# 16-head attention: TensorE's step for the next sequence's operands stands behind the diagonal scores, ahead of the values

## The chip, the cores and the metric

The kernel runs on one core of a Trainium2 chip. Its engines are TensorE (PE, with its weight loads shown apart as PEld), VectorE (DVE), ScalarE (ACT), GpSimd (POOL) and SyncE (SP), each with a program of its own; they meet at semaphores. The metric is the device time of one execution in microseconds (us). Of the kernel before, three runs gave 1028.70, 1028.92 and 1029.70 us, median 1028.92.

## The reference

Two transformer layers work on x of shape (8, 512, 128), each an attention and a feed-forward part with a normalisation in front and a gate behind. The change lies in the attention of the second layer, which has 16 heads of 8 channels:

```python
qkv = (x @ w_qkv.T + b_qkv).reshape(B, T, 3, H, dh)          # q, k, v per head
std_logits = einsum('bhqd,bhkd->bhqk', q, k) * scale
write_lines, read_lines = exterior(w1, w2), exterior(r1, r2)  # 6 numbers per head, divided by their norm
incidence = einsum('bqhp,bkhp->bhqk', read_lines, write_lines @ J6)
bias = incidence * decays ** (q - k) * (q > k) * bias_scale
attn = softmax(std_logits + bias, causal)
out  = einsum('bhqk,bhkd->bqhd', attn, v) @ w_out.T + b_out
```

## The kernel before, in words

The attention runs over 128 heads in a row (8 sequences of 16 heads). One pass of the loop over n is called slot n here; there are 152 slots (`LAST`), and a slot's place in its sequence is n mod 16. In slot n each engine works on head n for the maxima and on head j = n - 8 for the exponentials. TensorE's slot, in program order (lines 1728 to 1771):

1. `on_diagonal(n)` (L1630, L1631, L1633): scores on the diagonal. It waits until VectorE has weighted the incidences of head n (`weigh`, L1777).
2. `values` (L1693, waits for the exponentials), `turn_out` (L1701), and once per sequence `turn_rows` (L1716) and `project` (L1722). `values` comes in slots 1, 2 and 3 of every four, `turn_out` in slot 0 of every four, for groups of four heads.
3. `incidences_by_key(j)` (L1649). It waits for the exponentials of head j - 1 (L1858); VectorE's `weigh_by_key(j)` (L1782) waits for it.
4. `side(n)`: TensorE's step for the operands of the next sequence, one step of the generator `operands_pe`.
5. `below(n)` (L1641), `incidences(n + 1)` (L1623; VectorE's `weigh(n + 1)` waits for it), `on_diagonal_by_key(j)` (L1656 to L1659; it waits for `weigh_by_key(j)`, and ScalarE's exponentials L1857 and L1858 wait for it), `below_by_key(j + 1)` (L1668), `turn_maxima` (L1675).

VectorE's slot is `weigh(n)` L1777, maxima L1795, L1796, L1787, `weigh_by_key(j)` L1782, `normalise` L1808 and L1812, `residual` L1819, and its own side step last. ScalarE's side step stands first in its slot, GpSimd's near the front.

The operands of sequence b are made from slot 16b - 27 on. TensorE's steps with work in them, by n mod 16:

| n mod 16 | TensorE's step | who takes it |
|---|---|---|
| 9 | transposes of the normalised x (L1250) | ACT L1350 |
| 10, 11 | q, k (L1254, L1257) | ACT L1356, then POOL L1417, L1419 |
| 12 | v (L1261) | ACT L1361 |
| 13, 14 | line coordinates (L1271, L1272) | ACT L1369 (cp), then POOL L1434 on |
| 5 | transposes of half the lines (L1286), waits for GpSimd's L1402 | ACT L1375, then DVE L1326, in the same slot |
| 7 | transposes of the other half (L1286) | ACT L1378, then DVE L1330, L1331, in the same slot |

Between slot 14 and slot 5 GpSimd makes the lines from cp and divides them by their norms: products L1434 and L1435, differences L1442 to L1447, squares and sums L1451 to L1461, one VectorE hop (L1309, L1311, in VectorE's side step of slot 2 mod 16), Newton steps L1393 to L1397, product L1402. In the same program order it also does L1922, L1930 and L1907 to L1915. Sequences 0 and 1 are prepared in the first layer, except for the two L1286 steps of sequence 1 (slots 5 and 7). In the loop TensorE's side step therefore has work in 50 slots; 48 of them lie behind slot 8, that is behind the first `incidences_by_key`.

Of the kernel before, what the change touches and what calls it, by code (L numbers as in the profile page):

```python
# [36 lines left out]
def over(ap, n):  # L37
    return ap.rearrange("p (o c) -> p o c", o=1).to_broadcast([ap.shape[0], n, ap.shape[1]])
# [984 lines left out]
def attention1(c, t, sh, held):  # L1023
# [111 lines left out]
    def group_at(n, after):  # L1135

        q, r = divmod(n - after - G - LAG, G)
        return q if r == 0 and 0 <= q < GROUPS_ else None
# [8 lines left out]
    def rows_at(n, after):  # L1147
        return next((b for b in range(B) if rows_slot(b) + after == n), None)
# [426 lines left out]
    def main(late, behind):  # L1575
# [27 lines left out]
        def on_pe():  # L1603
            def block(x, n, a):

                i, h = place(n)
                return x[i][:, h * T + a * P:h * T + (a + 1) * P]
# [6 lines left out]
            def incidences(n):  # L1614


                if n % G == 0:
                    pe.wait_ge(s_fetch[n // G % RING], 64 * (n // H + 1))
                if n:
                    pe.wait_ge(s_ra, n)  # L1620
                for a in range(NT):
                    for z in HALVES:
                        m = pe.matmul(psD[z, a * P + HB:(a + 1) * P], block(QO, n, a)[:, z], block(KC, n, a)[:, z], start=a == 0, stop=False, skip_group_check=True)  # L1623
                m.then_inc(s_inc, 1)

            def on_diagonal(n):
                pe.wait_ge(s_wq, n + 1)
                for a in range(NT):
                    q, k = block(QO, n, a), block(KB, n, a)
                    pe.matmul(psD[HB:P, a * P:(a + 1) * P], q[:, HB:P], k, start=False, stop=False, skip_group_check=True)  # L1630
                    pe.matmul(psD[0:HB, a * P + HB:(a + 1) * P], q[:, 0:HB], k[:, 0:HB], start=False, stop=False, skip_group_check=True)  # L1631
                for z in HALVES:
                    m = pe.matmul(half(psD[z, :], 1), sh.identh[:, z], over(maskq, NT), start=False, stop=True, skip_group_check=True)  # L1633
                m.then_inc(s_own, 1)

            def below(n):
                if n:
                    pe.wait_ge(s_rc, n)
                i, h = place(n)
                for a, at in ROW_AT.items():  # L1640
                    m = pe.matmul(psX[:, at:at + a * P], block(QO, n, a), KA[i][:, h * KX + off[a]:h * KX + off[a + 1]], start=True, stop=True, skip_group_check=True)  # L1641
                m.then_inc(s_off, 1)

            def incidences_by_key(n):
                if n:
                    pe.wait_ge(s_expd, n)
                for a in range(NT):
                    for z in HALVES:
                        m = pe.matmul(psDT[z, a * P:a * P + HB], block(KC, n, a)[:, z], block(QO, n, a)[:, z], start=a == 0, stop=False, skip_group_check=True)  # L1649
                m.then_inc(s_incT, 1)  # L1650

            def on_diagonal_by_key(n):
                pe.wait_ge(s_wk, n + 1)
                for a in range(NT):
                    q, k = block(QO, n, a), block(KB, n, a)
                    pe.matmul(psDT[0:HB, a * P:(a + 1) * P], k[:, 0:HB], q, start=False, stop=False, skip_group_check=True)  # L1656
                    pe.matmul(psDT[HB:P, a * P:a * P + HB], k[:, HB:P], q[:, HB:P], start=False, stop=False, skip_group_check=True)
                for z in HALVES:
                    m = pe.matmul(half(psDT[z, :], 0), sh.identh[:, z], over(maskk, NT), start=False, stop=True, skip_group_check=True)  # L1659
                m.then_inc(s_ownT, 1)  # L1660

            def below_by_key(n):
                if n % G == 0:
                    pe.wait_ge(s_mset[n // G % 2], 16 * (n // G // 2 + 1))
                if n:
                    pe.wait_ge(s_expo, n)
                for x, (k, a) in enumerate(PAIRS):
                    m = pe.matmul(psXT[:, x * P:(x + 1) * P], decayed(n, k, a), block(QO, n, a), start=True, stop=True, skip_group_check=True)  # L1668
                m.then_inc(s_offT, 1)
# [7 lines left out]
            def values(q, k):  # L1677

                b = q // 4
                if q == 0:  # L1680
                    pe.wait_ge(s_edge, 1)
                if k == 0:
                    pe.wait_ge(s_expd, G * (q + 1))
                    pe.wait_ge(s_expo, G * (q + 1))
                    if q:
                        pe.wait_ge(s_O, q)
                at, first = k * P, NT + sum(NT - 1 - x for x in range(k))
                for c0, c1, e0 in ((at, at + P, at), (at + P, T, first * P)):
                    if c0 < c1:
                        for n in range(G * q, G * q + G):  # L1690
                            h = n % H
                            r, v0 = 32 * (h % 4), (k * H + h) * VH
                            m = pe.matmul(psO[r:r + 32, c0:c1], vv[b % NV][:, v0:v0 + 32], ET[n % NE][:, e0:e0 + c1 - c0],  # L1693
                                          start=c0 == 0, stop=k == NT - 1, skip_group_check=True)
                if k == NT - 1:
                    m.then_inc(s_pv, 1)

            def turn_out(q):
                pe.wait_ge(s_oS, q + 1)
                for i in range(NT):  # L1700
                    m = pe.transpose(psO[:, i * P:(i + 1) * P], oS[:, i * P:(i + 1) * P], sh.ident)  # L1701
                m.then_inc(s_oT, 1)

            def turn_rows(b):
                pe.wait_ge(s_O, 4 * b + 4)

                if b + 3 < B:
                    pe.wait_ge(s_cp, 2 * (b + 3) + 2)
                else:
                    pe.wait_ge(s_rawlo, 2 * B)  # L1710
                if b:
                    pe.wait_ge(s_Y, b)
                if b == B - 1:
                    pe.wait_ge(behind.s_seen, 1)
                for i in range(NT):
                    m = pe.transpose(psA[:, i * P:(i + 1) * P], O[:, i * P:(i + 1) * P], sh.ident)  # L1716
                m.then_inc(s_OT, 1)

            def project(b):
                pe.wait_ge(s_rows, b + 1)  # L1720
                for i in range(NT):
                    m = pe.matmul(psA[:, i * D:(i + 1) * D], oT[:, i * P:(i + 1) * P], wo, start=True, stop=True)  # L1722
                m.then_inc(s_proj, 1)

            side = ahead.pe
            pe.wait_ge(s_place, 1)
            incidences(0)
            for n in range(LAST):
                j = n - LAG
                if n < HEADS:  # L1730
                    on_diagonal(n)
                q = group_at(n, 1)
                if q is not None:
                    values(q, 0)
                q = group_at(n, 2)
                if q is not None:
                    values(q, 1)
                q = group_at(n, 3)
                if q is not None:
                    values(q, 2)  # L1740
                    values(q, 3)
                q = group_at(n, 4)
                if q is not None:
                    turn_out(q)
                b = rows_at(n, 0)
                if b is not None:
                    turn_rows(b)
                b = rows_at(n, 1)
                if b is not None:
                    project(b)  # L1750
                if 0 <= j < HEADS:
                    incidences_by_key(j)
                side(n)
                if n < HEADS:
                    below(n)
                if n + 1 < HEADS:
                    incidences(n + 1)
                if 0 <= j < HEADS:
                    on_diagonal_by_key(j)
                if 0 <= j + 1 < HEADS:  # L1760
                    below_by_key(j + 1)
                g, x = divmod(n - 5, G)
                if x == 0 and 0 <= g < GROUPS_:
                    turn_maxima(g)
                if n == behind.FLAG:

                    pe.wait_ge(s_Y, B - 1)
                if n == behind.ROWS:

                    pe.wait_ge(s_ra, HEADS)  # L1770
                behind.pe(n)
# [160 lines left out]

        on_sp()
        on_pe()
        on_dve()
        on_act()
# [377 lines left out]
```

## Time and profile before

| | |
|---|---|
| median of 3 runs | 1028.92 us (1028.70 to 1029.70) |
| profiled execution, its own time | 1027.37 us |
| its span, first to last instruction | 1026.1 us |
| PE busy | 857.4 us, 84% |
| DVE busy | 741.1 us, 72% |
| ACT busy | 656.5 us, 64% |
| POOL busy | 407.4 us, 40% |
| mean granted TensorE clock | 0.939 of full |

Busy shares are means over stages with different limits. The 16-head attention takes the stretch from about 320 to 830 us. Times in the rows below are counted from the first instruction. A timeline row has the start, the duration, the engine and line, the tiles, and in brackets the idle time of the engine before it and what ended it. Starts of matmul groups are firmer than their ends, so pieces are measured here from start to start. One sequence, slots 62 to 72, is followed throughout.

### The profile page before, as it was taken

How to read it: one execution, taken by the hardware profiler on the slowest of the kernel's cores; microseconds unless marked ns; L12 is line 12 of the kernel's file. 1: busy time of each engine (PE TensorE's matmuls, PEld its weight loads, DVE VectorE, ACT ScalarE, POOL GpSimd, SP SyncE). 2: the span in 40 equal slices, each digit the busy share in tenths (PEclk: the TensorE clock that was granted, in tenths of full speed). 3: DMA queues.
4: the chain of work that ended last, by engine and by line, in shares of the span. 5: the costliest groups of instructions: out<-in, count | busy, mean ns of one | idle time of the engine just before them, and what ended most of it. 6: DMA issues, size and time to landing. Idle time of an engine off the chain costs nothing.

```text
span 1026.1 us, 25492 instructions
## 1 busy us (share of the span) xinstructions
PE 857.4 (84%) x9999; PEld 532.0 (52%) x9999; DVE 741.1 (72%) x1794; ACT 656.5 (64%) x1154; POOL 407.4 (40%) x667
## 2 busy tenths in 40 slices
PE   4688888877376798989989899898898869898987
PEld 2344455545254465666656566565565534444434
DVE  4776888898886777677686867768688456656653
ACT  4668888747144465766666576766566738585865
POOL 3043555456557455384654637355032210101000
PEclk9899999989686699999999999999999989899999
DMA  5000000000333362533425244352532000000000
GB/s 150 22 0 1 1 1 1 1 1 2 106 88 98 78 171 58 133 103 95 127 68 160 62 116 127 76 155 63 150 107 66 2 1 1 21 2 21 1 22 21
DMA packets 70698, 63.60 MB, mean 62 GB/s; under 512 B 30600, under 2 KB 62824, under 8 KB 70576
## 3 DMA queue, kind: packets, MB, share of 16 engines
q1 hardware_dynamic: 70064, 61.90, 23.0%
q8 instruction: 83, 1.36, 0.6%
q14 instruction: 39, 0.32, 0.1%
q10 hardware_dynamic: 512, 0.02, 0.0%
HBM read 34.02 MB, written 27.36 MB: 60 GB/s over the span
## 4 chain that ended last, share of the span: by engine, by line
PE 37%; POOL 10%; DVE 9%; issue 6%; ACT 5%; SPq 1%; DMA 1%; POOLq 0%; DVEq 0%; ACTq 0%
PE bank L2115 12%; PE bank L1693 6%; PE bank L1668 2%; PE bank L1649 2%; PE bank L1641 2%; PE bank L1630 2%; POOL M L1434 2%; ACT 4g L2173 1%; POOL M L1435 1%; DVE bank L1777 1%; DVE 4f L2209 1%; PE bank L1623 1%; PE bank L1633 1%; POOL sq L1451 1%; PE bank L1659 1%
## 5 line engine op out<-in xcount | busy, mean ns | idle before, releaser
L1857 ACT ACTIVATE ET<-bank 64x512 f32<-64x512 f32 x128 | 75.5, 590 | 100.0 <-PE bank L1659 99.2
L2196 DVE TENSOR_TENSOR act<-4f,act 128x512 f16<-128x512 f32 x96 | 66.4, 691 | 57.7 <-ACT act L2163 57.5
L1852 ACT ACTIVATE ET<-bank 128x768 f32<-128x768 f32 x128 | 103.2, 806 | 2.4
L1777 DVE TENSOR_TENSOR bank<-bank,W 128x256 f32<-128x256 f32 x128 | 54.7, 427 | 52.7 <-PE bank L1623 52.7
L1693 PE MATMUL bank<-ET,vv 128*32 128x128 f32 (+2 forms) x1792 | 89.1, 323 | 0.8 <-DVE O L1812 0.8
L1787 DVE TENSOR_REDUCE mo<-bank 128x4 f32<-128x512 f32 x128 | 87.4, 683 | 2.4 <-PE bank L1633 2.3
L1782 DVE TENSOR_TENSOR bank<-bank,WT 128x256 f32<-128x256 f32 x128 | 55.1, 431 | 44.2 <-PE bank L1649 41.1
L2163 ACT ACTIVATE act<-4f 128x512 f16<-128x512 f32 x96 | 60.4, 630 | 28.3 <-DVE 4f L2209 26.2
L1795 DVE TENSOR_REDUCE mo<-bank 128x3 f32<-128x384 f32 x128 | 70.0, 547 | 0.0
L1796 DVE TENSOR_REDUCE mo<-bank 128x3 f32<-128x384 f32 x128 | 70.0, 547 | 0.0
L2115 PE MATMUL bank<-act,std 128*128 128x512 f16 x256 | 58.3, 390 | 0.0
L2115 PE MATMUL bank<-act,cp 128*128 128x512 f16 x256 | 56.5, 379 | 0.0
L1630 PE MATMUL bank<-ring 128*64 128x128 f16 x256 | 28.5, 239 | 32.1 <-DVE bank L1777 32.1
L1693 PEld LDWEIGHTS bank<-ET,vv 128*32 128x32 f32 x1792 | 43.6, 109 | 14.5 <-ACT ET L1858 1.0
L1858 ACT ACTIVATE ET<-bank 64x256 f32<-64x256 f32 x128 | 48.6, 380 | 1.5
L1633 PE MATMUL bank<-maskq,identh 128*64 128x256 bf16 x256 | 49.0, 286 | 0.0
L1434 POOL TENSOR_TENSOR M<-cp 128x192 f32<-128x192 f32 (+2 forms) x48 | 24.2, 505 | 61.6 <-ACT cp L1369 61.6
L1659 PE MATMUL bank<-maskk,identh 128*64 128x256 bf16 x256 | 48.0, 277 | 0.0
L2184 ACT ACTIVATE 4f<-bank,roots 128x512 f32<-128x512 f32 x64 | 43.3, 676 | 7.3 <-PE bank L2115 7.3
L2233 POOL TENSOR_TENSOR X<-X,4Y 128x512 f32<-128x512 f32 x8 | 10.1, 1265 | 91.6 <-DVE 4Y L2222 91.6
L139 POOL TENSOR_TENSOR rstd<-ve,neghalf 128x4 f32<-128x4 f32 x8 | 9.3, 1161 | 92.3 <-DVE ve L121 92.3
L2115 PEld LDWEIGHTS bank<-act,std 128*128 128x128 f16 x256 | 25.7, 101 | 31.4 <-issue 3.3
(384 smaller groups left out, 2544.8 us busy)
## 6 DMA issues: line engine op xcount, KB each, us to landing
ring<-scr_q SPq DMA_DIRECT2D x16, 324.0 KB
QO<-scr_q SPq DMA_DIRECT2D x16, 324.0 KB
ring<-scr_a SPq DMA_DIRECT2D x16, 252.0 KB
KA<-scr_a SPq DMA_DIRECT2D x16, 252.0 KB
ring<-scr_k SPq DMA_DIRECT2D x16, 168.0 KB
KB<-scr_k SPq DMA_DIRECT2D x16, 168.0 KB
scr_a<-dk SPq DMA_DIRECT2D x8, 288.0 KB, 2.6
X<-in_x SPq DMA_DIRECT2D x8, 256.0 KB, 5.1
```

Source lines behind the costliest of these rows:

```text
L1633: m = pe.matmul(half(psD[z, :], 1), sh.identh[:, z], over(maskq, NT), start=False, stop=True, skip_group_check=True)
L1659: m = pe.matmul(half(psDT[z, :], 0), sh.identh[:, z], over(maskk, NT), start=False, stop=True, skip_group_check=True)
L1693: m = pe.matmul(psO[r:r + 32, c0:c1], vv[b % NV][:, v0:v0 + 32], ET[n % NE][:, e0:e0 + c1 - c0], start=c0 == 0, stop=k == NT - 1, skip_gro ...
L1777: dve.tensor_tensor(half(psD, 1), half(psD, 1), over(W[:, h * HB:(h + 1) * HB], NT), ALU.mult).then_inc(s_wq, 1)
L1787: dve.tensor_reduce(tiles(mo[g % 2][:, x * NT * NT:(x + 1) * NT * NT])[:, :, NT - 1], tiles(psD), AX.X, ALU.max).then_inc(s_ra, 1)
L1795: dve.tensor_reduce(to[:, 12:15], tiles(psX[:, 0:3 * P], 3), AX.X, ALU.max).then_inc(s_rb, 1)
L1796: dve.tensor_reduce(to[:, 6:11:2], tiles(psX[:, 512:512 + 3 * P], 3), AX.X, ALU.max).then_inc(s_rc, 1)
L1852: act.activation(ET[n % NE][:, T:SEG * P], psXT[:, 0:NP * P], ACT.Exp).then_inc(s_expo, 1)
L1857: act.activation(to[0:HB, :], psDT[0:HB, :], ACT.Exp)
L2115: m = pe.matmul(to, l, r, start=n == 0, stop=n == len(todo) - 1)
L2163: act.activation(act_[s][layer % 2][0][:, o * T:(o + 1) * T], f32_[f % 3], ACT.Copy).then_inc(s_hi, 1)
L2196: dve.tensor_tensor(lo, f32_[f % 3], hi, ALU.subtract).then_inc(s_lo, 1)
```

## The change

The call `side(n)` of TensorE's program moves from step 4 of the slot to between steps 1 and 2. Nothing is added or removed, and the programs of the other engines stay the same.

```diff
                 if n < HEADS:
                     on_diagonal(n)
+                side(n)
                 q = group_at(n, 1)
                 if q is not None:
                     values(q, 0)
...
                 if 0 <= j < HEADS:
                     incidences_by_key(j)
-                side(n)
                 if n < HEADS:
                     below(n)
```

TensorE's program in a slot 5 mod 16, before. QO, KC, KB, KA and ring are the rings of fetched operands, ET the exponentials, vv the values, L the lines:

```order
L1633 MATMUL bank<-maskq,identh 64x4x64 x2
L1693 MATMUL bank<-ET,vv 32x128 x4
L1693 MATMUL bank<-ET,vv 32x384 x4
L1649 MATMUL bank<-QO,KC 64x64 x8
L1286 MATMUL bank<-ident,L 96x128 x4
L1641 MATMUL bank<-ring 128x384
```

and in the changed kernel:

```order
L1633 MATMUL bank<-maskq,identh 64x4x64 x2
L1286 MATMUL bank<-ident,L 96x128 x4
L1693 MATMUL bank<-ET,vv 32x128 x4
L1693 MATMUL bank<-ET,vv 32x384 x4
L1649 MATMUL bank<-QO,KC 64x64 x8
L1641 MATMUL bank<-ring 128x384
```

The transposes of the lines, with their wait for GpSimd, have moved ahead of the values and of the incidences by key.

TensorE's program in a slot 14 mod 16, before. 3hT is the normalised sequence, wl the weights of the lines:

```order
L1633 MATMUL bank<-maskq,identh 64x4x64 x2
L1693 MATMUL bank<-ET,vv 32x128 x4
L1693 MATMUL bank<-ET,vv 32x256 x4
L1649 MATMUL bank<-ring 64x64 x8
L1271 MATMUL bank<-wl,3hT 128x64
L1272 MATMUL bank<-wl,3hT 128x192
L1271 MATMUL bank<-wl,3hT 128x64
L1272 MATMUL bank<-wl,3hT 128x192
L1641 MATMUL bank<-KA,QO 128x384
```

and in the changed kernel:

```order
L1633 MATMUL bank<-maskq,identh 64x4x64 x2
L1271 MATMUL bank<-wl,3hT 128x64
L1272 MATMUL bank<-wl,3hT 128x192
L1271 MATMUL bank<-wl,3hT 128x64
L1272 MATMUL bank<-wl,3hT 128x192
L1693 MATMUL bank<-ET,vv 32x128 x4
L1693 MATMUL bank<-ET,vv 32x256 x4
L1649 MATMUL bank<-ring 64x64 x8
L1641 MATMUL bank<-KA,QO 128x384
```

The second half of the line coordinates, from which ScalarE makes cp, now stands ahead of the value matmuls and the incidences by key.

## Rows read from the trace of the kernel before

**Rows 1.** Busy time by stretch; (x) is a count, then granted clock, DMA.
```profile
400.00:740.00 340.00, 312.13 (x5676) 210.28 (x5676) 255.57 (x623) 220.75 (x404) 170.24 (x344) 1.00 0.42 107
```

**Rows 2.** Timeline, TensorE, slot 62 (14 mod 16): start, duration, engine, line.
```profile
554.80 0.86 PE L1693 MATMUL bank<-ET,vv 128*32 128x128 f32 x16
...
555.83 0.43 PE L1271 MATMUL bank<-wl,3hT 128*128 128x64 f32 x2
...
557.03 0.49 PE L1641 MATMUL bank<-KA,QO 128*128 128x384 f16 x3
...
558.03 0.51 PE L1668 MATMUL bank<-ring 128*128 128x128 f16 x6
```

**Rows 3.** Timeline, ScalarE, the same slot.
```profile
557.23 0.60 ACT L1369 ACTIVATE cp<-bank 128x512 f32<-128x512 f32 x1 [1.24 <-PE bank L1272]
```

**Rows 4.** Timeline, GpSimd, from cp to the divided lines.
```profile
557.91 0.59 POOL L1434 TENSOR_TENSOR M<-cp 128x192 f32<-128x192 f32 x1 [8.90 <-ACT cp L1369]
...
572.19 0.45 POOL L1461 TENSOR_TENSOR roots<-sq 128x128 f32<-128x128 f32 x1
...
579.05 1.82 POOL L1402 TENSOR_TENSOR L<-L,roots 128x768 f32<-128x768 f32 x1
```

**Rows 5.** Timeline, TensorE, slot 66 (2 mod 16) and the start of slot 67.
```profile
570.91 0.50 PE L1641 MATMUL bank<-ring 128*128 128x384 f16 x3
...
571.96 0.51 PE L1668 MATMUL bank<-QO,KA 128*128 128x128 f16 x6
573.56 0.24 PE L1630 MATMUL bank<-ring 128*64 128x128 f16 x1 [1.10 <-DVE bank L1777]
```

**Rows 6.** Timeline, VectorE, slots 66, 69 (5 mod 16) and 71 (7 mod 16).
```profile
572.68 0.23 DVE L1309 TENSOR_SCALAR roots<-roots 128x128 f32<-128x128 f32 x1 [1.23 <-POOL roots L1461]
...
573.08 0.43 DVE L1777 TENSOR_TENSOR bank<-bank,W 128x256 f32<-128x256 f32 x1
...
581.14 0.43 DVE L1782 TENSOR_TENSOR bank<-bank,WT 128x256 f32<-128x256 f32 x1 [0.41 <-PE bank L1649]
582.34 1.08 DVE L1326 TENSOR_TENSOR sq<-bank,Dk 96x128 f32<-96x128 f32 x3 [0.76 <-ACT raw L1375]
...
584.12 0.41 DVE L1777 TENSOR_TENSOR bank<-bank,W 128x256 f32<-128x256 f32 x1
...
590.08 0.43 DVE L1782 TENSOR_TENSOR bank<-bank,WT 128x256 f32<-128x256 f32 x1
591.27 0.69 DVE L1330 TENSOR_TENSOR cp<-bank,Dq 96x512 f32<-96x512 f32 x1 [0.76 <-ACT raw L1378]
...
592.21 0.42 DVE L1777 TENSOR_TENSOR bank<-bank,W 128x256 f32<-128x256 f32 x1
```

**Rows 7.** Timeline, TensorE, slot 69 (5 mod 16) and the start of slot 70.
```profile
579.78 1.07 PE L1693 MATMUL bank<-ET,vv 128*32 128x128 f32 x16
...
581.03 0.64 PE L1286 MATMUL bank<-ident,L 128*96 128x128 f32 x4
581.51 0.49 PE L1641 MATMUL bank<-ring 128*128 128x384 f16 x3
...
584.58 0.24 PE L1630 MATMUL bank<-ring 128*64 128x128 f16 x1 [1.40 <-DVE bank L1777]
```

**Rows 8.** Timeline, TensorE, slot 5, where the lines come late.
```profile
336.92 0.45 PE L1286 MATMUL bank<-ident,L 128*96 128x128 f32 x1 [0.99 <-POOL L L1402]
```

**Rows 9.** Timeline, TensorE, slots 9 and 10, where no values run yet.
```profile
353.30 0.32 PE L1649 MATMUL bank<-ring 128*64 128x64 f16 x8 [0.85 <-ACT ET L1858]
...
356.19 0.32 PE L1649 MATMUL bank<-ring 128*64 128x64 f16 x8 [0.18 <-ACT ET L1858]
```

**Rows 10.** Timeline, TensorE, start of slot 19.
```profile
388.02 0.24 PE L1630 MATMUL bank<-ring 128*64 128x128 f16 x1 [1.98 <-DVE bank L1777]
```

**Rows 11.** Busy time by stretch: slots 19 and 20, and 35 and 36 with the same work.
```profile
388.02:395.15 7.13, 7.13 (x118) 4.82 (x118) 5.51 (x14) 2.70 (x5) 6.15 (x13) 0.76 0.30 82
450.77:456.53 5.76, 5.76 (x118) 4.08 (x118) 5.31 (x14) 3.03 (x6) 4.78 (x13) 1.00 0.28 63
```

## The prediction

> **What bounds the kernel now.** I read the stretches first, then the timeline of one sequence. From 400 to 740 us TensorE is busy 312 of 340 us [rows 1], so the attention is TensorE's, and two things can move it: the 28 us in which it idles, and work done at the lower clock. The idle time is not spread evenly. Nearly all sits in front of L1630, the start of a slot, where TensorE waits for VectorE's L1777: 1.10 us behind slot 66, 1.40 us behind slot 69 [rows 5, 7]. Following back why VectorE is late gives two different answers.
>
> Behind slot 66 VectorE idles 1.23 us for GpSimd's L1461 [rows 6]. GpSimd began that work at 557.91, at once when ScalarE's cp arrived, after 8.90 us with nothing to do [rows 4], and from there to the end of L1402 at 580.87 it pauses only for VectorE's hop. So slot 2 of each sequence ends when cp arrived plus some 15 us that stay the same. And cp follows TensorE's L1272 at once [rows 3]: it is late because that step stands behind values and incidences.
>
> Behind slot 69 the chain is L1286 (581.03), ScalarE's copy, VectorE's L1326 (582.34), then L1777 (584.12) [rows 6, 7].
>
> **The change part by part.** I follow one sequence and write down by how much each point shifts; minus is earlier.
>
> Slots 9 to 14, TensorE's own cost. VectorE's L1782 waits for L1649, which now comes right ahead of L1641; before, the side step lay between them and hid it. From L1641 to L1668 it is 1.00 us in slot 62, with the side step as cover (558.03 - 557.03), and 1.05 us in slot 66, which has none (571.96 - 570.91) [rows 2, 5]. So each of these slots pays about 0.05 us; the side step itself costs the same in either place (1.20 us from L1271 to L1641 in slot 62 [rows 2]). What it costs between two f32 groups no row shows: for each I allow -0.05 to +0.15 us each, and take 0.05, the row's difference. In slot 9 this is offset by a wait of L1649 for the exponentials of about the same size. By the end of slot 13 the shift is +0.2, by the end of slot 14 +0.25.
>
> Slot 14, cp. L1271 moves ahead of values and incidences, 555.83 - 554.80 = 1.03 us [rows 2]. ScalarE idled 1.24 us there [rows 3], so it follows whole: cp shifts by +0.2 - 1.03 = -0.83, and GpSimd's whole run with it. Lower bound of the gain: none, if GpSimd would meet another wait (the maxima L1907 or the residual L1930). It meets none by more than a hair, as far as the order shows, so I take it whole.
>
> Slot 2. L1461 and L1777 come 0.83 us earlier than before. TensorE's own work would end 1.10 us before 573.56 [rows 5] and is itself 0.25 late, so slot 67 starts at -0.83: the slot gains 1.06 us, nearly all its stall.
>
> Slot 5, where it is paid back. L1402 ends at 580.87 - 0.83 = 580.04. TensorE reaches the place of L1286 at 579.78 - 0.83 = 578.95, waits 1.1 us, and starts it at 580.09 (0.05 us behind its releaser, as L1630 at 573.56 stands behind the end of L1777 at 573.51 [rows 5, 6]). Before, this wait was hidden: 1.25 us of values and incidences ran ahead of L1286 (581.03 - 579.78), and the lines were ready 0.16 us before they were wanted [rows 4, 7]. Now they are queued behind it: L1286 0.48 us (581.51 - 581.03), then 1.25 us, so that L1782 comes at 580.09 + 0.48 + 1.25 + 0.11 = 581.93 instead of 581.14 and ends at 582.36. ScalarE's copy is long done by then, so VectorE's L1326 starts at 582.3, as before [rows 6]. The slot ends at about -0.05: it takes 0.77 us more than before.
>
> Slot 7. L1286 starts 1.04 us earlier in the slot, and its inputs are there. But VectorE first does L1782, which is 0.48 us later: 590.56 to 590.99. Then L1330 and L1331, 592.21 - 591.27 = 0.94 us, and L1777 at 591.9 instead of 592.21 [rows 6]: 0.35 us gained. The other bound is 0.72 us, where TensorE's own work ends; it would need L1782 to be no longer ahead.
>
> A sequence comes to +0.25 - 1.06 + 0.77 - 0.35 = -0.4 us. There are five such (made in slots 25 to 103): -2.0 us.
>
> The first one (sequence 2, slots 9 to 23) differs. In slots 9 to 12 no values run, and TensorE idles for the exponentials, 0.85 us and then three times about 0.18, the first of which stands in the rows [rows 9]. The side step now fills these: about 0.45 of the first, as long as the transposes are, and the three whole: 1.0 us gained. Slots 13 and 14 cost 0.1, slot 23 gains 0.35. In slot 18 the stall is 1.98 us [rows 10], and cp takes 1.03 off it. After that stall slots 19 and 20 ran partly at the lower of the two clocks, 1.2 GHz: the two took 7.13 us at a granted clock of 0.76, slots 35 and 36 with the same work 5.76 us at 1.00 [rows 11]; that is 1.37 us. The stall left is under 1 us, shorter than the 1.40 us ones after which the clock stayed up [rows 7], so I count the 1.37 as gained, and slot 21 as paying 0.77. If the low clock stays, slot 21 has its lines in time and gains about 0.4 instead, so the two differ little. Sum of the first sequence: -1.0 + 0.1 - 1.03 - 1.37 + 0.77 - 0.35 = -2.9 us.
>
> Slots 5 and 7 of sequence 1 have nothing between the two places; the other four engines' programs, SP's queue of fetches with them, and all other stages stay as they are; TensorE issues no DMA. Total -4.9 us: 1027.37 becomes 1022.5 for a profiled execution. The median of the runs is 1.55 us above the profiled one, so I forecast 1024.0.
>
> **A rule against this change.** TensorE stood idle 0.99 us in front of L1286 in slot 5 while L1641, whose inputs were there, waited behind it [rows 8]. The Trainium skill (TensorE: Matmul & The Clock Gate, "Step-by-step: what each phase is for") says that weight loads may be pulled ahead but matmuls stay in program order; by that rule the values are held up in slot 5, and the trace agrees. Were it otherwise, six times 0.77 us would not be paid, and the sum would be -9.5 us.
>
> **Rivals.**
> (a) The values are not held up, or GpSimd's spans end later than the real ones do, so that slot 5 costs little: -9.5 us, 1019.4. Against it: row 8, in which matmul and span agree to 0.05 us. Chance 0.08.
> (b) Slower: the clock. Slot 5 now has two stalls, 1.1 us ahead of L1286 and 1.0 at its end, where there was one of 1.40. If these together bring TensorE to 1.2 GHz, each of six sequences pays what slots 19 and 20 paid, 1.37 us: +8.2 - 4.9 = +3.3, 1032.2. It decides from about 0.8 us per sequence. Against it: each stall is shorter than the one before, and 3 us of matmuls lie between them. The Trainium skill (same page, "What's actually happening") has activity releasing the throttle and idleness restoring it; the fall behind slot 18's stall agrees. Chance 0.07.
> (c) GpSimd's run does not move, because something else than cp holds it in slots 14 to 2: slot 2 gains nothing and slot 5 still pays. Then a sequence is +0.65, the first one -1.7 with the clock as it was: +1.6, 1030.5. Against it: the 8.90 us of idleness ended by cp. Chance 0.08.
> (d) The move costs more than 0.05 us per slot in slots 9 to 14, up to the 0.15 bound: 32 slots more at 0.1 each, +3.2, so -1.7 in all: no difference to be told, 1027.2. Chance 0.12.
>
> **How the numbers follow.** The forecast, -3 to -7 us, has 0.65. What a measurement of this kernel can tell from no change is about 0.2%, 2.1 us. Faster by more takes the forecast, (a) and a little of (d): 0.75. Within: most of (d), part of (c): 0.15. Slower: (b), part of (c): 0.10. The forecast's own range is 1022 to 1026; to hold 8 in 10 it reaches to (a) and past (d): 1019.8 to 1028.4.
>
> **What would show it.** VectorE's wait for L1461 in slots 2 mod 16 nearly gone, and TensorE's 1.10 us behind them; GpSimd's L1434 about 1 us earlier in slot 14. Slots 5 mod 16 longer by 0.75 us, with a new wait of PE L1286 for POOL L1402 of about 1.1 us, five or six times. Slots 7 mod 16 shorter by 0.35. Slots 9 to 12 each shorter by 0.2 to 0.45 in the first round only. Full clock in slot 19. The prediction is wrong if slot 5 does not grow, if slot 2 keeps its stall, or if slots 9 to 14 of later sequences change by more than 0.15 us each.

## The result, and the profile after

The changed kernel took 1026.30 us (median of 14 runs, 1021.51 to 1029.34), the kernel before 1029.22 us beside it (median of 14, 1028.11 to 1032.51). The ratio is 0.9966 with a 95% interval of 0.9953 to 0.9979: 2.9 us at these medians, faster by 0.34%. The forecast was 1024.0 us, -4.9, with 1022 to 1026 as its own range (-3 to -7) and 1019.8 to 1028.4 as the wide one. The measured time lies 0.3 us above the first and inside the second. The direction and the waits of slots 2, 5 and 7 held, and the size was 2 us too large. In the five repeated sequences the change costs time instead of gaining it.

| | before | after |
|---|---|---|
| profiled execution, its own time | 1027.37 | 1026.84 |
| span | 1026.1 | 1025.6 |
| PE busy | 857.4 | 862.0 |
| mean granted TensorE clock | 0.939 | 0.943 |
| attention begins (first L1630) | 321.82 | 323.66 |
| from there to the start of slot 126 | 470.64 | 468.03 |

The two profiled executions differ by only 0.5 us, because the stages in front of the attention ended 1.8 us later in the second. From the start of the attention to slot 126 the gain is 2.61 us in this profile and 3.07 us in a second one of the same kernel. So I read the attention in slots, each from one first L1630 to the next. Up to slot 110, slot lengths differ by 0.01 us between the two profiles of the changed kernel (in slots 18 and 34 by 0.02 to 0.03), while the start of the attention lies anywhere between 321.6 and 327.8 us over the kernels of this study. The table has the medians of slots 25 to 104.

| slot mod 16 | before | after | difference | predicted |
|---|---|---|---|---|
| 9 | 3.72 | 3.78 | +0.06 | 0.05 less a wait |
| 10 | 3.88 | 4.03 | +0.15 | +0.05 |
| 11 | 3.89 | 4.04 | +0.15 | +0.05 |
| 12 | 3.71 | 3.71 | 0 | +0.05 |
| 13 | 4.34 | 4.49 | +0.15 | +0.05 |
| 14 | 4.12 | 4.27 | +0.15 | +0.05 |
| 2 | 4.13 | 3.05 | -1.09 | -1.06 |
| 5 | 5.25 | 6.09 | +0.84 | +0.77 |
| 7 | 4.20 | 3.92 | -0.29 | -0.35 |

All others keep their length to 0.01 us, up to slot 110. A sequence comes to +0.11 us instead of -0.4, the five to +0.6 us (slots 25 to 104) instead of -2.0: in the repeated part the change is a small loss. The first one, slots 8 to 24, gained 2.5 us instead of 2.9, and 1.36 of it is the clock in slots 19 and 20.

Up to slot 110, where all terms of the forecast lie, the change thus gained 1.9 us in this profile and 2.0 in the second, 40% of the forecast. Slot 111, where TensorE waits for fetched operands, and those behind it gave the rest, -0.7 us here and -1.1 us in the second profile. That was in no term of the sum. Slot 111 alone takes anything from 5.60 to 7.47 us over the profiles of this study, so it is not shown that this part comes from the change. That the total came so near to the forecast is in part luck.

TensorE in slot 62 of the changed kernel (start, duration, engine, line), beside [rows 2]:

```profile
554.90 0.43 PE L1271 MATMUL bank<-wl,3hT 128*128 128x64 f32 x2
...
556.19 0.86 PE L1693 MATMUL bank<-ET,vv 128*32 128x128 f32 x16
...
557.23 0.50 PE L1641 MATMUL bank<-KA,QO 128*128 128x384 f16 x3
...
558.28 0.51 PE L1668 MATMUL bank<-ring 128*128 128x128 f16 x6
```

The step from L1271 now takes 556.19 - 554.90 = 1.29 us where it took 1.20, and from L1641 to L1668 it is 1.05 us instead of 1.00. These are the slot's +0.15, in two parts.

ScalarE's cp in the same slot, beside [rows 3]:

```profile
556.30 0.60 ACT L1369 ACTIVATE cp<-bank 128x512 f32<-128x512 f32 x1 [0.21 <-PE bank L1272]
```

GpSimd from cp to the divided lines, beside [rows 4]:

```profile
556.97 0.59 POOL L1434 TENSOR_TENSOR M<-cp 128x192 f32<-128x192 f32 x1 [8.35 <-ACT cp L1369]
...
571.36 0.46 POOL L1461 TENSOR_TENSOR roots<-sq 128x128 f32<-128x128 f32 x1
...
578.22 1.80 POOL L1402 TENSOR_TENSOR L<-L,roots 128x768 f32<-128x768 f32 x1
```

Starts on the two traces differ by where the sequence began, too: slot 57 starts at 534.40 here and at 534.81 before. Counted from there, cp is 0.93 - 0.41 = 0.52 us earlier and L1461 0.83 - 0.41 = 0.42 us, where 0.83 was predicted for both. Inside slot 62 the step moved by the 1.03 us that were foreseen, but slots 9 to 13 had put it 0.51 us behind, not 0.2. VectorE takes it up in slot 66, beside [rows 6]:

```profile
571.85 0.23 DVE L1309 TENSOR_SCALAR roots<-roots 128x128 f32<-128x128 f32 x1
...
572.25 0.42 DVE L1777 TENSOR_TENSOR bank<-bank,W 128x256 f32<-128x256 f32 x1
```

The 1.23 us of idle time for L1461 is gone, and slot 67 begins at TensorE's own pace, without the 1.10 us wait of [rows 5]:

```profile
572.21 0.51 PE L1668 MATMUL bank<-QO,KA 128*128 128x128 f16 x6
572.73 0.24 PE L1630 MATMUL bank<-ring 128*64 128x128 f16 x1
```

The payment, TensorE in slot 69, beside [rows 7]:

```profile
578.50 0.24 PE L1630 MATMUL bank<-ring 128*64 128x128 f16 x1
...
580.08 0.64 PE L1286 MATMUL bank<-ident,L 128*96 128x128 f32 x4 [1.06 <-POOL L L1402]
580.65 1.07 PE L1693 MATMUL bank<-ET,vv 128*32 128x128 f32 x16
...
581.90 0.50 PE L1641 MATMUL bank<-ring 128*128 128x384 f16 x3
...
584.59 0.24 PE L1630 MATMUL bank<-ring 128*64 128x128 f16 x1 [0.97 <-DVE bank L1777]
```

The new wait is the 1.1 us that was foreseen, and the values stand behind it. (Slot 101 has less work than the other slots 5 and grew by the same 0.84 us, from 4.48 to 5.31.) VectorE in slots 69 and 71, beside [rows 6]:

```profile
582.01 0.43 DVE L1782 TENSOR_TENSOR bank<-bank,WT 128x256 f32<-128x256 f32 x1 [2.12 <-PE bank L1649]
582.35 1.07 DVE L1326 TENSOR_TENSOR sq<-bank,Dk 96x128 f32<-96x128 f32 x3
...
584.12 0.41 DVE L1777 TENSOR_TENSOR bank<-bank,W 128x256 f32<-128x256 f32 x1
...
590.66 0.43 DVE L1782 TENSOR_TENSOR bank<-bank,WT 128x256 f32<-128x256 f32 x1 [0.71 <-PE bank L1649]
591.00 0.68 DVE L1330 TENSOR_TENSOR cp<-bank,Dq 96x512 f32<-96x512 f32 x1
...
591.93 0.42 DVE L1777 TENSOR_TENSOR bank<-bank,W 128x256 f32<-128x256 f32 x1
```

L1777 for slot 70 stands at 584.12 in both traces. Counted from slot 57 that is 0.41 us late, where the prediction had it 0.05 us early: the lead of 0.42 us at slot 67 is spent twice over.

Busy time by stretch, first slots 19 and 20, beside [rows 11], then the stretch of [rows 1]:

```profile
388.20:393.97 5.77, 5.77 (x119) 4.09 (x120) 5.32 (x14) 3.32 (x6) 4.79 (x13) 1.00 0.24 75
400.00:740.00 340.00, 317.41 (x5676) 209.51 (x5676) 254.06 (x621) 221.38 (x404) 170.53 (x344) 1.00 0.41 107
```

Slots 19 and 20 ran at the full clock and took 5.77 us instead of 7.13. Over the 340 us the same 5676 matmuls keep TensorE busy 5.3 us longer at the same clock. The busy share rose and no more was done: the idle time that went was paid out as longer matmul groups, and as short waits inside them that this view counts as busy. TensorE's waits in that stretch (total us, times, longest us), before:

```profile
PE bank L1630 <- DVE bank L1777: 27.0, 34, 1.4
```

and after:

```profile
PE bank L1630 <- DVE bank L1777: 16.3, 29, 1.0
PE bank L1286 <- POOL L L1402: 5.3, 5, 1.1
```

10.7 us of one wait went and 5.3 us of another came; the difference of 5.4 us is the longer busy time.

### The profile page after: what moved, and what is told of

The parts are those of the page before. It is cut to its first block, busy times and chain, and to the rows that moved or that the text cites. A ratio compares the mean times of both kernels' runs of the same rounds, so it can differ in the third digit from the quotient of the medians.

```text
span 1025.6 us, 25492 instructions
## 1 busy us (share of the span) xinstructions
PE 862.0 (84%) x9999; PEld 529.8 (52%) x9999; DVE 740.0 (72%) x1794; ACT 656.5 (64%) x1154; POOL 407.6 (40%) x667
## 3 DMA queue, kind: packets, MB, share of 16 engines
q8 instruction: 83, 1.36, 0.6%
## 4 chain that ended last, share of the span: by engine, by line
PE 33%; POOL 14%; DVE 9%; issue 8%; ACT 4%; POOLq 0%; DVEq 0%; ACTq 0%
PE bank L2115 12%; PE bank L1693 5%; PE bank L1668 2%; POOL roots L1393 2%; PE bank L1641 2%; POOL M L1434 2%; PE bank L1649 2%; ACT 4g L2173 1%; PE bank L1630 1%; POOL M L1435 1%; DVE 4f L2209 1%; POOL L L1402 1%; DVE bank L1777 1%; POOL sq L1451 1%; POOL roots L1397 1%
## 5 line engine op out<-in xcount | busy, mean ns | idle before, releaser
L1782 DVE TENSOR_TENSOR bank<-bank,WT 128x256 f32<-128x256 f32 x128 | 55.1, 431 | 92.6 <-PE bank L1649 90.4
L1693 PE MATMUL bank<-ET,vv 128*32 128x128 f32 (+2 forms) x1792 | 90.1, 326 | 0.8 <-DVE O L1812 0.8
L1777 DVE TENSOR_TENSOR bank<-bank,W 128x256 f32<-128x256 f32 x128 | 54.6, 427 | 19.6 <-PE bank L1623 19.6
L1693 PEld LDWEIGHTS bank<-ET,vv 128*32 128x32 f32 x1792 | 44.0, 110 | 22.3 <-issue 12.8
L1858 ACT ACTIVATE ET<-bank 64x256 f32<-64x256 f32 x128 | 48.4, 378 | 1.5
L1630 PE MATMUL bank<-ring 128*64 128x128 f16 x256 | 28.1, 236 | 23.8 <-DVE bank L1777 23.8
```

The costliest lines, as they stand in the source:

```text
L1777: dve.tensor_tensor(half(psD, 1), half(psD, 1), over(W[:, h * HB:(h + 1) * HB], NT), ALU.mult).then_inc(s_wq, 1)
L1782: dve.tensor_tensor(half(psDT, 0), half(psDT, 0), over(WT[:, h * HB:(h + 1) * HB], NT), ALU.mult).then_inc(s_wk, 1)
```

## The experiments

In the diffs `side(n)` ahead of the values is the new place, the one ahead of `below(n)` the old one. Each edit is made to the kernel before unless it says otherwise. The conditions shift the line numbers by 3: L1780, L1785 and L1910 there are L1777, L1782 and L1907. Ratios are against the kernel before on the same chip.

### All steps moved but the one of slot 5

```diff
+                if n % H != 5:
+                    side(n)
...
-                side(n)
+                if n % H == 5:
+                    side(n)
```

> The changed kernel, but in slots 5 mod 16 TensorE's side step (L1286, which waits for GpSimd's L1402) stays in its old place. Theory: in those slots the values are queued behind the wait for the lines, which costs 0.84 us in each of six; without it slots 5 are 5.25 us again and the kernel comes 5.0 us below the changed one, near 1021 to 1022. Rival (the gain of the move is small for another reason, slot 5 is only where VectorE's lateness shows): slots 5 stay at 6.1 us or the time turns up in slots 6 to 8, and the kernel stays near 1026.

Measured: 1020.88 us against 1029.01 (ratio 0.9928, 0.9907 to 0.9949). Slots 5 are back at 5.25, slots 2 stay at 3.05, slots 7 at 3.92, and to the start of slot 126 it gained 7.16 us (6.97 up to slot 110, where the changed kernel has 1.9). The step in slot 5 alone takes away more than half of what the change could bring.

### Only the step of slot 14 moved

```diff
+                if n % H == 14:
+                    side(n)
...
-                side(n)
+                if n % H != 14:
+                    side(n)
```

> The kernel before, with only the side step of slots 14 mod 16 (second half of the line coordinates, from which cp is made) moved ahead of the values. Theory: this step alone carries the gain: slot 14 costs 0.15 us, slot 2 gains 1.08 in each of six sequences, and slots 19 and 20 run at the full clock (1.36): -7.0 us, about 1022. L1286 stays behind values and incidences, where the lines are ready in time for it to within 0.1 us. Rival (GpSimd's run is set by something earlier, such as the first half of the coordinates in slot 13, so that cp of slot 14 alone is not enough): slot 2 keeps most of its stall and the time stays within 1 us of before.

Measured: 1022.35 us against 1029.01 (0.9932, 0.9912 to 0.9952). Slots 2 are 3.05, slot 18 is 3.84 and slots 19 and 20 run at full clock; slots 14 cost 0.15, slots 10, 11 and 13 nothing. It gained 7.0 us up to slot 126. So cp carries the gain, and this one step of the six suffices for it.

### Only the step of slot 5 moved

```diff
+                if n % H == 5:
+                    side(n)
...
-                side(n)
+                if n % H != 5:
+                    side(n)
```

> The kernel before, with only the side step of slots 5 mod 16 moved. Theory: the lines are no earlier than before, so TensorE waits 1.1 us ahead of L1286 with the values behind it, and slots 37, 53, 69, 85, 101 become 0.84 us longer; in slot 21 the lines are early (the slots before it ran at the lower clock) and it gains 0.3: +3.9 us, about 1033. Rival (VectorE gets its lines earlier and gains as much as the values lose): no difference, 1029.

Measured: 1033.14 us against 1029.01 (1.0038, 1.0022 to 1.0054): slower by 0.2% at least. TensorE in its slot 69:

```profile
584.45 0.64 PE L1286 MATMUL bank<-ident,L 128*96 128x128 f32 x4 [1.05 <-POOL L L1402]
```

The wait of 1.05 us is there whether cp is early or not, and slots 5 take 6.08 us (6.09 in the changed kernel). Slot 21, where the lines were early, gained 0.29 us by the same move, as expected. The reading: slot 67 and L1402 both hang on GpSimd's run, L1461 first and L1402 6.9 us later (578.22 - 571.36 in the changed kernel), so an earlier cp moves both and the distance stays.

### The changed kernel once more

> The changed kernel once more, for a second profile and on the same chip as its parts. Theory: slots 10, 11, 13, 14 mod 16 are again 0.15 us longer than before, slots 5 0.84 longer, slots 2 1.08 shorter; the spread of its times (1021.5 to 1029.3) comes from stretches outside these slots, above all from where the lower clock falls. Rival: the slots themselves differ from execution to execution, so a second profile shows other lengths.

Measured: 1025.66 us against 1029.01 (0.9974, 0.9958 to 0.9990). All slots up to 110 have the length of the first profile to 0.01 us, slots 18 and 34 to 0.02 or 0.03. The two ratios together put the change at 0.3% faster.

### The steps of slots 9 to 14 between values and incidences by key

```diff
+                if 9 <= n % H <= 14:
+                    side(n)
                 if 0 <= j < HEADS:
                     incidences_by_key(j)
-                side(n)
+                if not 9 <= n % H <= 14:
+                    side(n)
```

> The kernel before, with the side steps of slots 9 to 14 mod 16 placed between the values and the incidences by key. It takes apart the 0.15 us that slots 10, 11, 13 and 14 cost in the changed kernel. Theory: 0.09 of it is the f32 side step standing right ahead of the f32 values (L1693 starts 1.06 us behind L1254 where L1641 did 0.97), 0.06 the bared wait for VectorE's L1782; here only the second is left, and these slots are 0.06 us longer than before. Rival (all of it is the bared wait): 0.15 again. In slot 2 the stall shrinks by only 0.25 us, since cp passes the incidences alone. About 1028, 1 us below before.

Measured: 1027.66 us against 1028.77 (0.9988, 0.9973 to 1.0002). The time came as expected; the reason for the slots' cost did not. The step in slot 58 at its three places: before,

```profile
539.76 0.32 PE L1649 MATMUL bank<-ring 128*64 128x64 f16 x8
540.01 1.12 PE L1254 MATMUL bank<-3hT,3wqkv 128*128 128x512 f32 x2
540.97 0.49 PE L1641 MATMUL bank<-KA,QO 128*128 128x384 f16 x3
```

changed kernel,

```profile
538.63 1.13 PE L1254 MATMUL bank<-3hT,3wqkv 128*128 128x512 f32 x2
539.69 0.86 PE L1693 MATMUL bank<-ET,vv 128*32 128x128 f32 x16
540.48 0.32 PE L1649 MATMUL bank<-ring 128*64 128x64 f16 x8
```

and here:

```profile
541.47 0.86 PE L1693 MATMUL bank<-ET,vv 128*32 128x128 f32 x16
542.26 1.13 PE L1254 MATMUL bank<-3hT,3wqkv 128*128 128x512 f32 x2
543.32 0.32 PE L1649 MATMUL bank<-ring 128*64 128x64 f16 x8
```

From start to start the same step takes 0.96, 1.06 and 1.06 us. My explanation was that an f32 group ahead of another f32 group costs the 0.1 us. It fell, since the group behind is f16 here and the cost is the same. Slots 10, 11, 13 and 14 again take 0.15 us more. That is the rival's number, but not for its reason: 0.10 of it lies in the step, ahead of any wait for L1782.

TensorE's weight loads (PEld) tell the three places apart. The first load of the group behind the step, before:

```profile
540.54 0.10 PEld L1641 LDWEIGHTS bank<-KA,QO 128*128 128x128 f16 x1 [0.24 <-issue]
```

changed kernel:

```profile
539.69 0.38 PEld L1693 LDWEIGHTS bank<-ET,vv 128*32 128x32 f32 x16 [0.76 <-issue]
```

and here:

```profile
543.32 0.20 PEld L1649 LDWEIGHTS bank<-ring 128*64 128x64 f16 x8 [0.76 <-issue]
```

Before, the load starts 0.43 us ahead of its matmul (540.97), while the step's last matmul runs. In the other two it starts only with its matmul, and the step's last matmul takes 0.52 us from start to start instead of 0.43. In the first case the step and the group behind it use the array in one form, 128*128. In the other two the form changes, to 128*32 or 128*64. Slot 2 gained 0.39 us (3.74), 0.14 more than expected.

### The changed kernel with GpSimd's residual bias moved away from slot 0

```diff
-                if x == 0 and b < B:
+                if x == 6 and b < B:
```

> The changed kernel, with GpSimd's 1.23 us L1922 moved from slot 0 mod 16, where it stands inside the run from cp to the lines, to slot 6 mod 16, behind that run. Theory: the lines are ready 1.2 us earlier, L1286 in slots 5 no longer waits, and the slot falls from 6.09 to 4.96 us, which the only-slot-5 kernel shows for slot 21, where the lines were early; slot 2 keeps 3.05. Six times 1.12: 6.7 us below the changed kernel, about 1019. Rival (the wait is not GpSimd's run but something bound to the slots): slot 5 stays at 6.1 and the time at 1026.

Measured: 1025.30 us against 1028.77 (0.9960, 0.9945 to 0.9975), and slots 5 still at 6.09: the expectation failed. GpSimd in slot 64, with the work taken away in front of it:

```profile
566.82 0.25 POOL L1910 TENSOR_SCALAR mleft<-mx 128x16 f32<-128x16 f32 x1 [1.29 <-DVE mx L1804]
```

GpSimd waits 1.29 us for VectorE's maxima of that slot and goes on with the lines only then. In the changed kernel the same instruction follows the maxima at once:

```profile
562.97 0.22 DVE L1801 TENSOR_REDUCE mx<-mo 128x16 f32<-128x64 f32 x1
...
563.28 0.25 POOL L1907 TENSOR_SCALAR mleft<-mx 128x16 f32<-128x16 f32 x1
```

So GpSimd's run is pinned at slot 0: the earlier cp had used up all that could be gained there, within 0.1 us. The forecast's remark that it meets no other wait "by more than a hair" was just true. Slot 18, in the first sequence, did gain 0.5 us more by this edit (3.35 us against 3.85).

### The steps of slots 7 and 14 moved, and those of slots without values

```diff
+                if n % H in (7, 14) or n < 13:
+                    side(n)
...
-                side(n)
+                if not (n % H in (7, 14) or n < 13):
+                    side(n)
```

> The kernel before, with only those side steps moved that gain by it: slots 7 and 14 mod 16, and all below slot 13, where no values run yet. Theory, from the slots measured so far: per sequence +0.15 - 1.08 - 0.28 = -1.21, five times; the first -0.8 + 0.15 - 1.17 - 1.36 - 0.28 = -3.5; in all -9.5 us, about 1019.6. Rival (the terms do not add): above 1021.

Measured: 1018.24 us against 1028.77 (0.9908, 0.9889 to 0.9928), the fastest of the study; the same kernel is run once more below. Up to slot 110 it gained 9.9 us. It keeps each gain of the change and pays none of its costs but the 0.15 us in slots 14. TensorE in slot 69, where L1286 is back behind values and incidences and waits for nothing:

```profile
572.12 0.24 PE L1630 MATMUL bank<-ring 128*64 128x128 f16 x1
...
572.58 1.07 PE L1693 MATMUL bank<-ET,vv 128*32 128x128 f32 x16
573.58 0.32 PE L1649 MATMUL bank<-QO,KC 128*64 128x64 f16 x8
573.82 0.64 PE L1286 MATMUL bank<-ident,L 128*96 128x128 f32 x4
...
577.37 0.24 PE L1630 MATMUL bank<-ring 128*64 128x128 f16 x1 [1.40 <-DVE bank L1780]
```

Slots 9 are 0.09 us shorter than before in this kernel. L1649 waited there for the exponentials L1858, which before ended at 536.29, with L1649 at 536.34, 1.54 us into the slot. Here they end 0.6 us ahead of it, since ScalarE's L1344 is done earlier, and L1649 comes at 1.45 us.

### Steps of slots 5, 7 and 14 moved, with the bias moved too

```diff
+                if n % H in (5, 7, 14) or n < 13:
+                    side(n)
...
-                side(n)
+                if not (n % H in (5, 7, 14) or n < 13):
+                    side(n)
...
-                if x == 0 and b < B:
+                if x == 6 and b < B:
```

> As the kernel with steps 7 and 14, with L1922 in slot 6 mod 16 and the side step of slots 5 moved too. Theory: with the lines early, the move in slot 5 turns from a loss of 0.84 us into a gain of 0.29, and slot 2 loses its last 0.07: 2.0 us below the kernel with steps 7 and 14, about 1017.6. Rival (slot 5 loses by the move whatever the lines do): above 1021.

Measured: 1020.99 us against 1028.77 (0.9933, 0.9920 to 0.9946). Slots 5 take 6.11 us, with a wait of 1.08 us for L1402. It missed for the same reason as the one with the bias alone.

### The changed kernel with two Newton steps

```diff
-        for i in range(3):
+        for i in range(2):
```

The semaphore counts of the steps change with it.

> The changed kernel with the third Newton step of the norms left out (about 1.9 us of GpSimd's run; the norms are coarser for it). Moving L1922 had not made the lines earlier, since GpSimd then waits for VectorE's maxima in slot 0; this takes time out behind that wait and behind VectorE's hop in slot 2. Theory: L1402 ends 1.9 us earlier, L1286 in slots 5 mod 16 starts without a wait, and the slot falls from 6.09 to 4.96 us; slot 2 stays at 3.05: six times 1.13, 6.8 us below the changed kernel, about 1019. Rival (slot 5 is long whatever the lines do): 6.1 us again, 1026.

Measured: 1019.34 us against 1029.28 (0.9913, 0.9895 to 0.9931). TensorE in slot 69, with the lines ready 1 us before they are wanted:

```profile
575.09 0.24 PE L1630 MATMUL bank<-ring 128*64 128x128 f16 x1
...
575.54 0.64 PE L1286 MATMUL bank<-ident,L 128*96 128x128 f32 x4
576.11 1.07 PE L1693 MATMUL bank<-ET,vv 128*32 128x128 f32 x16
...
580.05 0.24 PE L1630 MATMUL bank<-ring 128*64 128x128 f16 x1 [0.96 <-DVE bank L1777]
```

L1286 stands at the new place and waits for nothing, and the slot takes 4.96 us, 0.29 less than before the change instead of 0.84 more. The early place is good in itself; what costs is the wait for L1402. The computation lacks a Newton step, so this is no candidate.

### The steps of slots 5 and 7 between values and incidences by key

```diff
+                if n % H == 14 or n < 13:
+                    side(n)
                 q = group_at(n, 1)
...
+                if n % H in (5, 7) and n >= 13:
+                    side(n)
                 if 0 <= j < HEADS:
                     incidences_by_key(j)
```

The old place takes all others.

> As the kernel with steps 7 and 14, but the side steps of slots 5 and 7 mod 16 stand between the values and the incidences by key, so that in slot 5 the values run while the lines are waited for. Theory: in slot 5 L1286 starts at 1.58 instead of 1.70 us, ScalarE's copy ends at 2.85, and the slot is 5.11 us (5.25 before, 6.09 in the changed kernel); slot 7 is 3.92 as when moved ahead of the values. 0.8 us below the kernel with steps 7 and 14, about 1017.4. Rival (VectorE's L1782, which is then later, takes it back): 5.25 or more, no difference to that kernel.

Measured: 1019.95 us against 1029.28 (0.9906, 0.9888 to 0.9924). Slots 5 take 5.15 and slots 7 3.96 us, 0.04 us above the expectation each. Against the kernel of the next heading slots 5 gain 0.10 us, but slots 7 lose 0.04 and slots 9 lose 0.09 (3.72 against 3.63). With L1286 of slot 7 in the middle ScalarE is late again in slot 9, and L1649 waits for the exponentials as before. Nothing is left of the gain: both kernels are 10.0 us shorter than before up to slot 110, and 1019.95 and 1020.19 us are not told apart.

### Steps 7 and 14 again, beside the last

The edit is that of the steps of slots 7 and 14 above.

> The kernel with steps 7 and 14 (and those below slot 13) once more, on the chip of its variant with steps 5 and 7 in the middle. Theory: 1018 to 1019 again, slots 5 mod 16 5.25 us.

Measured: 1020.19 us against 1029.28 (0.9916, 0.9901 to 0.9932). The gain of 9 us of the first run of this edit stands; up to slot 110 it is 10.0 us here and was 9.9 there.

### The steps of slots 9 to 14 behind the scores below the diagonal

```diff
-                side(n)
+                if not 9 <= n % H <= 14:
+                    side(n)
                 if n < HEADS:
                     below(n)
+                if 9 <= n % H <= 14:
+                    side(n)
```

> The kernel before, with the side steps of slots 9 to 14 mod 16 placed one place later, behind L1641 instead of ahead of it: one look at what neighbours cost. Behind L1641 (128 columns) the side step took 0.97 us in slot 10, ahead of L1693 (32 columns) and of L1649 (64 columns) 1.06 and 1.05. Theory: the 0.09 us is paid where a group on part of the array follows the side step; here L1623 (64 columns) follows it, but L1641 then lies ahead of the side step, not ahead of L1623, so the switch that L1641 to L1623 had is moved, not added, and L1649 still has its cover: slots 10, 11, 13, 14 as before (3.88, 3.89, 4.34, 4.12). Rival (each side step ahead of a group on part of the array costs 0.09 by itself): 0.09 us longer each.

Measured, in one run: 1033.12 us. Slots 9 to 14 take 3.69, 3.80, 3.80, 3.77, 4.25 and 4.03 us, all but slot 12 shorter than before, by 0.02 to 0.09. Neither the theory nor the rival had that. (The expectation says "behind L1641" of the step before; it stood ahead of L1641.) TensorE's loads in slot 58, and the step itself:

```profile
542.86 0.30 PEld L1254 LDWEIGHTS bank<-3hT,3wqkv 128*128 128x128 f32 x2
...
543.91 0.20 PEld L1623 LDWEIGHTS bank<-KC,QO 128*64 128x64 f16 x8 [0.76 <-issue]
```

```profile
542.96 1.02 PE L1254 MATMUL bank<-3hT,3wqkv 128*128 128x512 f32 x2
```

Now the step's own first load starts 0.11 us ahead of its matmul, under L1641, and its first matmul takes 0.43 us instead of 0.53. L1641's last matmul is shorter too, by 0.09 us. In return L1623's load comes late and the step's last matmul is 0.52 us again. Two savings and one loss against before make the slot 0.09 us shorter. Slot 12 has the same saving, but L1649 waits there for the exponentials L1858 until 549.91, which costs 0.14 us. What lengthened the kernel is cp, which now comes later: slots 2 take 4.47 us (+0.33). In sequence 64 to 79 that stall had a second effect, on the clock. TensorE at the start of slot 67, and the stretch of that slot:

```profile
576.21 0.25 PE L1630 MATMUL bank<-ring 128*64 128x128 f16 x1 [1.43 <-DVE bank L1780]
```

```profile
576.21:580.58 4.37, 4.37 (x70) 2.87 (x71) 2.60 (x6) 0.93 (x2) 3.63 (x10) 0.61 0.00 0
```

The granted clock is 0.61 and the slot takes 4.37 us instead of 2.98. Behind the stalls of the same length in slots 34, 50, 82 and 98 the next slot took its 2.98 us.

## Why the prediction was right, and where its size was wrong

**Slot 14 and slot 2** held: the step moved 1.03 us up in slot 14, and slot 2 lost its stall, -1.09 against -1.06. With the step of slot 14 alone moved the gain is all there, which shows the cause.

**Slot 5** held in place and kind. The wait was 1.06 us against 1.1, with the releaser named. Undoing this step gives slot 5 back (5.25), doing it alone produces it (6.09), and making the lines ready early removes it (4.96). The rule of the Trainium skill on program order (TensorE: Matmul & The Clock Gate, "Step-by-step: what each phase is for") is borne out here: the values, whose inputs were there, started only 0.57 us behind L1286; in the run with the lines ready they started 1.1 us earlier in the slot (576.11 - 575.09 against 580.65 - 578.50). The term was +0.77 and measured +0.84, mostly because L1286 to L1693 is 0.57 us where L1286 to L1641 was 0.48.

**Slot 7** was -0.35 and measured -0.29. It has the same 0.09 us in it, since L1330 waits behind L1782 and that behind L1649.

**Slots 9 to 14** are the term that was mis-sized. "The side step itself costs the same in either place" was the sentence that failed. Of the +0.15 us, 0.05 is the bared wait that was counted (L1641 to L1668, 1.05 us against 1.00), and about 0.10 is the step itself, 1.06 us against 0.96 in slot 58 and 1.29 against 1.20 in slot 62. No row of before showed the step between such neighbours. The range that was written down, -0.05 to +0.15, held, and its upper end was the truth in four slots of six; a little more and the forecast would have been wrong by its own test. Slot 12, where `turn_out` follows, cost nothing, and slot 9 0.06.

The traces show where the 0.10 us comes from. Between two groups that both use the array as 128*128 (or one of them as 128*96, as L1286 does), the first load of the second group starts ahead of its first matmul, by 0.05 to 0.43 us at all 932 such places in slots 8 to 119 of the fourteen traces. Where the form changes between 128*128, 128*96, 128*64, 128*48 and 128*32, it is never more than 0.005 us ahead, at 10112 places. Before, the step and L1641 were two groups of one form in a row, and the step's last matmul took 0.43 us. The new place puts L1693 (128*32) behind it, and it takes 0.52. The rest is 0.01 us in L1641, whose own first load is now late. In slot 12 the group behind is L1701, 128*128 again: its first matmul got 0.05 us shorter, which pays for L1641's 0.01 and the bared wait. In slots 5 and 7 it is the same 0.09 us, L1286 to the next group 0.57 us instead of 0.48.

In the sum: (4 x 0.15 + 0.06) - 0.25 = +0.4 a sequence, five times, is +2.0; 0.3 instead of 0.1 in slots 13 and 14 of the first sequence +0.2; six times 0.07 for slot 5 and six times 0.06 for slot 7 +0.8; slots 9 to 12 of the first sequence gained 0.8 instead of 1.0, +0.2. Slot 18 gained 1.18 instead of 1.03, and slots 2 five times 0.03 more, -0.3 together. From -4.9 that makes -2.0 up to slot 110, where the two profiles show -1.9 and -2.0. Slots 111 on gave 0.7 to 1.1 that were not counted, for no reason that the forecast had.

**The first sequence** held: slot 9 -0.46, slots 10 to 12 -0.11 each (-0.18 was expected), slots 19 and 20 back at full clock, -1.36 against -1.37.

**The rivals.** (a) fell: slot 5 costs 0.84 us. (b) fell: with two stalls of about 1 us in each slot 5 the granted clock is 1.00 over the whole stretch. (c) fell, though GpSimd's run has only some 0.1 us left before it meets the maxima. (d) was the right mechanism in part. Its bound holds in four slots of six and not in slots 9 and 12. The total lies between it and the forecast, and up to slot 110 the gain of 1.9 to 2.0 us is nearly (d)'s 1.7.

**What stays open.** The reading of the loads was taken from traces of kernels that were made for other questions. It fits slots 9 to 14 in each of them, the version behind `below` with its shorter slots among them, but no kernel was built to test it. What sets the length of slot 111 is open too.

## What to carry to other kernels

A step that moves to the front of a slot does two things: its consumer starts earlier, and everything behind it waits for its producer. Ask both questions for each slot in which the step has work, not once for the step. Here one of its eight places in a sequence carried nearly the whole gain (slot 14), one took most of it back (slot 5), and a placement by slot was worth 9 us where the uniform one was worth 3. Where a term rests on "costs the same elsewhere", multiply the bound by the number of instances before the middle is taken: 0.1 us in 22 slots was most of the error here. When a matmul group is moved, look at which groups it stood between: a neighbour that used the whole array too let a load start early here, worth about 0.1 us. And sum the repeated part by itself: a gain in the total can come from the first round alone, as it did here.

A change of 0.3% drowns in the scatter of one profiled execution. Lengths of a repeated slot, start to start, gave each term to 0.01 us.

## What the runs showed of the hardware that was not expected

- The same matmul group of slot 58 took 0.96 or 1.06 us by what stood beside it, and added 0.86 us between L1641 and L1623 in the version behind `below` (1.29 us from the one to the other, 0.43 us without it), all at a granted clock of 1.00. What went with it was whether the neighbour used the array as 128*128 too, so that a weight load could start ahead of its matmul.
- How long TensorE had stalled did not alone decide whether the clock fell. Behind the 1.98 us of [rows 10] and the 1.43 us shown above it did, though not behind four more stalls of that length in the same run. Behind 1.40 us [rows 7] it did not, nor behind these 1.57 us in front of slot 19 of the version between values and incidences, where slot 19 took 2.98 us:

```profile
391.38 0.24 PE L1630 MATMUL bank<-ring 128*64 128x128 f16 x1 [1.57 <-DVE bank L1780]
```

- Start to start, slots that an edit does not touch repeat to 0.01 us over kernels and chips where the clock is the same, while what lies in front of the attention ends anywhere in 6 us. Slot 111, which waits for fetched operands, took 5.60 to 7.47 us, and what lies behind slot 126 took 230.9 to 233.9 us.
